# Shared gate-up weights split inside cross attention's last batch, and the router's choice of experts put ahead of the shared unit

## What the kernel computes

```python
shared = jax.nn.silu(x @ Ws_gate) * (x @ Ws_up) @ Ws_down           # 512 -> 704 -> 512
scores = jax.nn.softmax(x @ W_router, axis=-1)                      # 8 experts
topk_vals, topk_idx = jax.lax.top_k(scores, 2)
combine = jnp.einsum('bsk,bske->bse', topk_vals, one_hot(topk_idx)) # weights of 2048 tokens
h = silu(einsum('td,edh->eth', xf, We_gate)) * einsum('td,edh->eth', xf, We_up)   # 352 wide
routed = einsum('etd,te->td', einsum('eth,ehd->etd', h, We_down), combine)
```

## Time and profile before

| | |
|---|---|
| median of three runs | 1088.21 us (1085.95 to 1089.79) |
| the profiled execution | 1088.47 us, of it 1086.8 us span |
| TensorE busy | 1016.1 us, 93% of the span |
| VectorE, ScalarE, GpSimd busy | 666.1, 456.7, 275.8 us |
| TensorE's granted clock | 0.974 of full speed, mean |
| cross attention's last batch | from about 512 to 551 us |
| `route` | 551.2 to 640.0 us |
| `experts`, `combine` | from 640.0 and from 927.7 us |

### The profile page before, as it was taken

How to read it: one execution, slowest core, us unless ns; L and a number is a source line. 1 busy time by engine, 2 the same in 40 slices (tenths; PEclk the granted TensorE clock), 3 DMA queues, 4 the chain that set the end, 5 groups by cost and what they waited for, 6 DMA issues and landing times. The chain is left out here.

```text
span 1086.8 us, 18081 instructions
## 1 busy us (share of the span) xinstructions
PE 1016.1 (93%) x6368; PEld 858.2 (79%) x6368; DVE 666.1 (61%) x1502; ACT 456.7 (42%) x798; POOL 275.8 (25%) x367
## 2 busy tenths in 40 slices
PE   7899999999979999999859979999999999899997
PEld 5688888888778888887637768888998889778785
DVE  4836556477265776776444847776777776253576
ACT  5623314145125544454443226555655664221110
POOL 4510100213143323333343122212231220503040
PEclk9999999999978999999998979999999999999999
DMA  5403032023877888884432157787778773615042
GB/s 168 180 1 116 0 115 87 0 81 126 205 187 194 212 228 239 218 219 131 171 99 81 63 179 225 252 256 266 243 246 277 251 244 113 213 40 188 6 155 77
DMA packets 87183, 172.66 MB, mean 159 GB/s; under 512 B 8112, under 2 KB 36016, under 8 KB 85328
## 3 DMA queue, kind: packets, MB, share of 16 engines
q1 hardware_dynamic: 81008, 150.08, 44.6%
q0 software_dynamic: 6112, 21.76, 6.1%
HBM read 130.92 MB, written 37.49 MB: 155 GB/s over the span
## 5 line engine op out<-in xcount | busy, mean ns | idle before, releaser
L45 PE MATMUL e_ps_h<-e_x_lo,e_gu_hi 128*128 128x256 f32 (+1 forms) x384 | 111.3, 290 | 10.8 <-DVE e_x_lo L2141 8.7
L45 PE MATMUL a_ps_proj<-region_a_rounded,arena 128*128 128x512 f32 x272 | 107.4, 395 | 11.2 <-DVE region_a_rounded L369 6.2
L953 DVE CUSTOM_DVE_ANT_0 b_dump<-b_ps_s,b_mask 128x128 f32<-128x128 f32 (+1 forms) x256 | 80.4, 354 | 46.5 <-PE b_ps_s L1143 43.3
L47 PE MATMUL e_ps_h<-e_x_hi,e_gu_hi 128*128 128x256 f32 (+1 forms) x384 | 108.2, 282 | 0.0
L46 PE MATMUL e_ps_h<-e_x_hi,e_gu_lo 128*128 128x256 f32 (+1 forms) x384 | 108.2, 282 | 0.0
L46 PE MATMUL a_ps_proj<-region_a_rounded,arena 128*128 128x512 f32 x272 | 106.4, 391 | 0.0
L47 PE MATMUL a_ps_proj<-region_a_rounded,arena 128*128 128x512 f32 x272 | 106.4, 391 | 0.0
L2147 DVE TENSOR_TENSOR e_gu_lo<-f_region_a,e_gu_hi 128x704 fp32r<-128x704 f32 x92 | 81.3, 889 | 26.8 <-ACT e_gu_hi L2057 26.3
L388 DVE SCALAR_TENSOR_TENSOR f_region_b<-a_ps_proj,a_taps,f_region_b 128x510 f32<-128x510 f32 (+2 forms) x96 | 71.7, 746 | 40.8 <-ACT f_region_b L328 38.5
L843 ACT ACTIVATE b_pt<-b_ps_x 128x384 f32<-128x384 f32 x128 | 61.8, 487 | 61.2 <-PE b_ps_x L1167 61.1
L757 POOL TENSOR_SCALAR_AFFINE_SELECT b_pt<-b_pt 128x256 f32<-128x256 f32 x128 | 51.8, 407 | 122.6 <-ACT b_pt L843 121.9
(11 more groups left out here) (400 smaller groups left out, 2693.7 us busy)
## 6 DMA issues: line engine op xcount, KB each, us to landing
f_region_a<-we_gate_up SPq DMA_DIRECT2D x88, 352.0 KB, 5.6
qk_split<-arena SPq DMA_DIRECT2D x24, 512.0 KB, 5.8
y_slots<-f_region_b SPq DMA_DIRECT2D x16, 512.0 KB, 3.4
f_x_next<-x SPq DMA_DIRECT2D x7, 1024.0 KB, 7.1
b_sk<-qk_split SPq DMA_DIRECT2D x24, 256.0 KB, 4.4
b_sq<-qk_split SPq DMA_DIRECT2D x24, 256.0 KB, 5.7
f_region_a<-we_down SPq DMA_DIRECT2D x12, 512.0 KB, 4.0
f_region_b<-we_down SPq DMA_DIRECT2D x11, 512.0 KB, 4.0
```

Of the source, the lines that this page charges most:

```text
L45: pe.matmul(out, a_hi, b_lo, start=first, stop=False)
L47: return pe.matmul(out, a_hi, b_hi, start=False, stop=last)
L953: ins = dve.tensor_tensor_reduce(dump[:, n % 2, cols], ps_s[:, n % 2, cols], mask[:, cols], -1.0, 3e38, ALU.add, ALU.min, peak[:, u, k, i: ...
```

## The change

Shared weights no longer have room of their own before `route`; they are laid over cross attention's arena, at places whose old content (query weights, key and value weights, split tiles) is dead when each is written. With that:

- SP, in batch 7, waits for batch 6's last scores, then issues shared parts 0 and 1 and both groups of x2, ahead of the store of batch 5's rows and of batch 7's peaks. Parts 2 and 3 follow behind the batch.
- ACT rounds parts 0 and 1 behind batch 7's last exponent, ahead of `keep`, and part 2 at the end. POOL takes their rests behind its last mask. Part 3 is rounded in `route` at (0, 1), and POOL takes its rest ahead of the constants but behind the root of the variance.
- The constants are waited for later, the first down part is fetched at `route`'s start.
- DVE picks both experts before it does unit 0's product; the counts follow unit 1 and not unit 2; units 1 to 3 are done within the chain of small instructions, unit 4 behind `hot_lo`, unit 5 behind `hot_hi` and its two multiplications, all adds behind that; the one-hot products stand ahead of down tile 2, not 3.
- The three table loads are taken out.

```diff
@@ cross_attention, SP
             for t in range(FIRST_T, END_T):
                 b = projected(t)
+                if t == B - 1:
+                    sp.wait_ge(e_ready, order(B - 2, 1, UH - 1) + 1)
+                    shared.load_part(sp, 0)
+                    shared.load_part(sp, 1)
+                    sp.wait_ge(xkq_ready, x_count(B - 1, 1))
+                    sp.wait_ge(normed_stored, 16 + 16 * (t - 2))
+                    sp.dma_start(xt[:], x2_dram[0]).then_inc(inputs_loaded[0], 16)
+                    sp.dma_start(own_b[:, 0:4 * GT]..., x2_dram[1]).then_inc(inputs_loaded[0], 16)
...
+            shared.load_part(sp, 2)
+            shared.load_part(sp, 3)
@@ cross_attention, POOL, at the end
+            for k in range(3):
+                shared.rest_part(pool, k)
@@ cross_attention, ACT
+                if t == B - 1:
+                    shared.round_part(act, 0)
+                    shared.round_part(act, 1)
                 keep(t)
             for u in range(2):
                 attended(B - 1, u)
+            shared.round_part(act, 2)
@@ Shared
+    def load_part(self, sp, k):
+        if k >= 2:
+            sp.wait_ge(self.part_lo_done, k - 1)
...
+    def round_part(self, act, k):
+        act.wait_ge(self.part_loaded[k % 2], 16 * (k // 2) + 16)
+        act.activation(hi, self.w_part[rows, k % 2, 0:cols], ACT.Copy).then_inc(self.part_hi_done, 1)
+    def rest_part(self, pool, k):
+        pool.wait_ge(self.part_hi_done, k + 1)
...
+        pool.tensor_tensor(lo, self.w_part[...], hi.bitcast(F32), ALU.subtract).then_inc(self.part_lo_done, 1)
@@ route, SP
             sp.dma_start(w_raw[:], w_router).then_inc(w_loaded, 16)
+            shared.load_part(sp, SPLIT + 1)
@@ route, POOL
             pool.memset(w_hi_lo[:].bitcast(F32), 0.0).then_inc(consts, 1)
+            pool.wait_ge(var_done, 1)
+            pool.tensor_tensor(ln.rstd[:], ln.var[:], ln.power[:], ALU.pow).then_inc(rstd_done, 1)
+            shared.rest_part(pool, SPLIT)
             pool.memset(before[:], 1.0).then_inc(consts, 1)
...
@@ route, ACT
-            act.preload_act_table_set("exp_and_others")
...
-                    if (g, c) in PARTS_AT:
-                        split_part(PARTS_AT[g, c])
+                    if g == 0 and c == 1:
+                        shared.round_part(act, SPLIT)
@@ route, DVE
-            shared.up(dve, 0, 0)
+            dve.wait_ge(iotas, 14)
...
             dve.tensor_tensor(both[:], pick[:, 0], pick[:, 1], ALU.add).then_inc(sub_both_done, 1)
-            shared.up(dve, 0, 1)
-            shared.up(dve, 0, 2)
+            shared.up(dve, 0, 0)
...
             link(dve.tensor_tensor(hot_lo[:], ...))
+            shared.up(dve, 0, 4)
             link(dve.tensor_tensor(hot_hi[:], ...))
-            dve.wait_ge(x2_stored, 16)
-            shared.add(dve, kept, 0, 0)
             for k in range(2):
                 rows = hot_hi[:, k * NT:(k + 1) * NT]
...
+            shared.up(dve, 0, 5)
+            dve.wait_ge(x2_stored, 16)
+            for t in range(TILES):
+                if t == 2:
                     dve.wait_ge(placed, 1)
@@ route, PE
-                if u == 2:
+                if u == 1:
                     pe.wait_ge(sub_both_done, 2)
...
-                if t == TILES - 1:
+                if t == 2:
                     pe.wait_ge(hot_done, 2)
@@ experts, ACT; combine, ACT
-            act.preload_act_table_set("silu_and_others")
```

More of the change, by code:

```diff
@@ L515, in cross_attention @@
 def cross_attention(nc, x1_dram, ctx_t, weights, x2_dram, left_ln, ident, xt, c_raw, res, ln, spare, c_hi, c_lo, split_dram,
-                    rounded, own_a, own_b, ws_gate_up):
+                    rounded, own_a, own_b, shared):
     with ExitStack() as ctx:
@@ L735, in _ @@
                     load_stack(t + 2, 1)
-            sp.wait_ge(xkq_ready, x_count(B - 1, 1))
+            shared.load_part(sp, 2)
+            shared.load_part(sp, 3)
             sp.wait_ge(normed_stored, 16 + 16 * NORMED)
[L738 to L744, removed]
+            sp.wait_ge(inputs_loaded[0], 32 * (GROUPS - 2) + 32)
         @block.gpsimd
@@ L1306, with __init__ @@
 class Shared:
-    def __init__(self, sb, sem):
+    ROOM = 2 * DC * 2 * DS + 2 * S_UNITS * D + 2 * 3 * P + P
+    def __init__(self, room, w_part, w_gate_up, w_down, sem):
         U = S_UNITS
[L1313 to L1316, removed]
+        chunk, down = [P, 2 * DS], [P, U, D]
+        hi, lo = [None] * DC, [None] * DC
+        hi[0], lo[0] = room("s_gu_hi_0", chunk), room("s_gu_lo_0", chunk)
+        self.dn_hi = room("s_dn_hi", down)
+        hi[3] = room("s_gu_hi_3", chunk)
+        self.small_hi, self.small_lo = room("e_small_hi", [P, 3, P]), room("e_small_lo", [P, 3, P])
+        room("s_gap", [P, P])
+        for c in (1, 2):
+            hi[c], lo[c] = room("s_gu_hi_%d" % c, chunk), room("s_gu_lo_%d" % c, chunk)
+        lo[3] = room("s_gu_lo_3", chunk)
+        self.dn_lo = room("s_dn_lo", down)
+        self.gu_hi, self.gu_lo = hi, lo
+        self.w_part = w_part
+        self.parts = self.list_parts(w_gate_up, w_down)
+        self.part_loaded = [sem("s_part_loaded_even"), sem("s_part_loaded_odd")]
+        self.part_hi_done = sem("s_part_hi_done")
+        self.part_lo_done = sem("s_part_lo_done")
         self.x_ready = sem("s_x_ready")
@@ L1326, in __init__, with list_parts @@
         self.out_free = sem("s_out_free")
-    def parts(self, w_gate_up, w_down):
+    def list_parts(self, w_gate_up, w_down):
         every = slice(0, P)
-        out = [(self.gu_hi[:, c], self.gu_lo[:, c], every, 2 * DS, w_gate_up[:, c]) for c in range(DC)]
+        out = [(self.gu_hi[c], self.gu_lo[c], every, 2 * DS, w_gate_up[:, c]) for c in range(DC)]
         for u in (0, 2):
@@ L1608, in _ @@
                 n += 2
[L1609 to L1613, removed]
+            for k in range(SPLIT + 1, S_PARTS):
+                shared.rest_part(pool, k)
             pool.wait_ge(token_known, 1)
@@ L1649, in _ @@
                 if DC + u < S_PARTS:
-                    split_part(DC + u)
+                    shared.round_part(act, DC + u)
         @block.vector
@@ L1730, in of_experts @@
                 return row.rearrange("p (o e) -> p o e", o=1).broadcast_to([P, NT, E_N])
+            shared.product(dve, 0, 1)
             link(dve.tensor_scalar(odd_base[:], first[:, 1], twice[:], float(P), ALU.add, ALU.mult))
@@ L1735, in _ @@
             link(dve.tensor_tensor(spill[:], spill[:], odd_base[:], ALU.subtract))
+            shared.rest(dve, 0, 1)
             link(dve.scalar_tensor_tensor(spill[:], spill[:], -float(SLOTS * SINGLES), over[:], ALU.add, ALU.mult))
@@ L1747, in _ @@
             link(dve.tensor_tensor(pos[:], pos[:], cand[:], ALU.add))
+            shared.product(dve, 0, 2)
             for k in range(2):
@@ L1750, in _ @@
                 link(dve.tensor_reduce(slot_f[:, k], cand[:], AX_X, ALU.add))
+            shared.rest(dve, 0, 2)
             def of_turns(x):
@@ L1756, in of_ends @@
                 return ends[:, k].rearrange("p (o e) -> p o e", o=1).broadcast_to([P, E_TILES + 1, E_N])
-            shared.product(dve, 0, 3)
             link(dve.tensor_copy(rt.slot[:], slot_f[:]))
```

80 lines of the change are left out of this document (34 added, 46 removed).

## The result

The change makes the kernel slower by 6.1 us. Before: 1087.56 us, median of 13 runs (1084.29 to 1091.32). After: 1093.64 us, median of 13 (1090.25 to 1098.44). The ratio is 1.0059, interval 1.0039 to 1.0079. The profiled execution of the changed kernel took 1091.24 us (span 1089.5). The forecast was 1088.6 us, "same", range to 1092.5: 5.0 us too low, and 1.1 us outside the range.

A forecast was written before the change was run, and what follows sets the result against it. TensorE was busy 93% of the span, but ScalarE's queue and a DMA ended last in the router. Terms +3.0 - 5.5 + 4.6 - 1.2 - 0.5 = +0.4 on 1088.2 gave 1088.6 us, range 1082.5 to 1092.5.

The forecast's parts named there:

- r_lo and tail: Cross attention's tail: GpSimd's queued second rest holds VectorE's r_lo to 540.9 for 537.9, +3.0 us.
- router: Router stage: x's rounding no longer waits, but a rest delays the normalisations; hidden units start 5.5 us earlier.
- hidden units to experts: First hidden product to the next block: 62.3 us for 57.75, through units 4 and 5's new place, +4.6 us.
- table load, experts: Load removed before the experts' first weight rounding: -1.2 of its 1.28 us arrives.
- table load, combine: Load removed in combine, where the first chunks are turned by 928.9: -0.5 of 1.28 us arrives.
- the locks: GpSimd's rests hold VectorE operations with two SBUF inputs or normalising: terms of 3.0, 2.4 and 4.4 us.
- one low stretch at 1.5 us: Down tile: TensorE at low clock after its gap, first eight products 3.5 us for 1.9, added as 1.5 us.
- the 5.76 us: TensorE gap in the old router, behind ScalarE's queue, where a rounding waited for a transfer 5.02 us too late.
- 62.3 us: First hidden product to the next block: 60.8 us plus 1.5 for low clock, against 57.75 before.
- VectorE's chain: Shared stage, counts to hot rows: starts 13.5 us after the first hidden product, ends 33.1 to 33.2, before 37.7.
- "+6": Upper bound of the term from hidden units to experts, with two low stretches, where the forecast was +4.6 us.
- rival (a): GpSimd gives way: queued rests wait for VectorE, the three lock terms go, -9.4, 1079.2 us; chance 0.31.

The follow-up runs named there:

- the fillings: Changed kernel with unread TensorE products inside waits: down tile's two 1089.4 us (ratio 1.0024), router's 1088.45 us (1.0003), both 1084.86 us (0.9971).

## Why the prediction was wrong

Against the mean of three profiles each, the terms of the sum came out so:

```
                              forecast   measured
r_lo and tail                   +3.0       +4.5
router                          -5.5       -4.3
hidden units to experts         +4.6       +6.0
table load, experts             -1.2       -1.3
table load, combine             -0.5       -0.6
sum                             +0.4       +4.3
experts' stage itself            0         +2.0
```

The signs were right in every line, and so were the locks, the waits and the gaps. Two steps failed. The low clock behind the new waits was put at nothing for r_lo's and the router's, and at too little in the down tile. And the lengths of the kernel before came from one execution.

**The clock behind new waits.** I priced one low stretch at 1.5 us, behind unit 5, from the row of a wait of 1.85 us, and none behind r_lo's wait or the router's. In the router the forecast was 25.5 us from its first product to the first hidden one; with the wait filled it takes just that, 25.50, and unfilled 26.6 to 28.0. So the lock's own cost there was right and the low clock of 1.1 to 2.5 us was missing. In the down tile the clock costs 2.83 us for the forecast 1.5. By the times of whole kernels the fillings gave 3.0, 5.3 and together 8.8 us, each with 3 us of uncertainty. Behind r_lo's wait the changed kernel has 6.8 low us in all three profiles (0.80 in its first window), the kernel before 3.4, 0 and 0; this one was not filled. With r_lo's lock taken away the tail takes 14.5 us, 1.7 more than the kernel before on the mean, of which `a_lo`'s meeting with part 1's rest explains 0.8; the rest, beside a low stretch of 3.4 us, is not separated. The forecast's own rows held the warning, since eight products at the low level stand behind the 5.76 us.

**The base.** The lengths came from one execution, the best one could do then, but I took the waits and low stretches in it as belonging to the kernel. Two more profiles show the same stages 2.9 us shorter. From the first hidden product to `experts` I forecast 62.3 us, and measured were 62.0, 63.6 and 62.0; it was compared with 57.8, while the other two profiles have 56.0. Likewise the tail: with a base of 12.2 the changed kernel loses 5.1 us and not 3.5.

**Luck.** The 62.3 is closer than its parts. VectorE's chain was to reach hot_lo 33.1 us behind the first hidden product and unit 5's rest to end at 44.7; in the first profile they come at 31.0 and 42.6, because the chain's first copy starts at 11.9 and not 13.5 and the rest of the chain is a little shorter too. From unit 5's rest to `experts` it takes 19.4 us and not 17.6, mostly for the clock. The two errors cancel. The rise of 6.0 us in this term is also the "+6" which the prediction gave for two low stretches, but it comes from the base.

**The locks** were forecast well: r_lo +3.0 (3.0), the normalisations to 4.60 us, the rests of parts 5 to 7 in the chain 2.1 + 1.1 + 1.0 = 4.2 us (4.3). Holding GpSimd back at r_lo and at the normalisations removes the first two; the three in the chain are read from the rows alone, where each held operation ends with a rest. The Trainium skill's rule ("SBUF — State Buffer", "Who interferes with whom") therefore held, and rival (a), GpSimd gives way, is refuted. Its time was also added up wrong: 9.4 below 1088.2 is 1078.8 us, and the 1079.2 counts the +0.4 twice.

**What stays open.** The mean span of the changed kernel's three profiles is 5.7 us longer, near the 6.1 of the medians. It is not 4.3 + 2.0 alone: what stands ahead of r_lo is 0.5 longer, and `combine` as a whole 1.7 shorter, of which only 0.6 is in the table above. The +2.0 in the experts' stage has no cause that I could show. Its instructions are the same, and over all profiles it took 281.2 to 288.5 us, the kernels with a filled wait at 281.2 to 282.5, but that with the table loads at 281.8 too, and that with r_lo freed at 288.5. Three profiles of each are too few to call it part of the change. The share of the table loads is known only as 1.6 to 2.9 us.

## What to carry to other kernels

Work moved to an idle engine is not free when its operations hold up those of a busy one: give GpSimd's long subtractions a wait that lets VectorE's next critical operation pass first, as the two waits here did, which cost two lines.
A new wait of TensorE can cost more than its length, by the low clock behind it: here 2.8 us behind two waits of 3.3 and 4.1 us, and 1.1 to 2.5 us in the router behind one of 4.8. Where a wait can't be removed, products that nobody reads can keep the clock.
Before adding up seams of a few us, profile the same kernel more than once: three identical executions differed by 2.9 us in the very stages that decided this case.

## What had not been expected of the hardware

Products into an unused PSUM bank, 19 in a wait of 4.76 us and 30 in waits of 3.28 and 4.13, made the kernel 8.8 us faster by the ratios, with 3 us of uncertainty, although no left-over came sooner by them (TensorE could take up unit 5 42.7 us behind the first hidden product in the changed kernel, and 45.5 in the kernel with the down tile filled, whose hidden units had a low stretch of their own).
Operations of 8 and 24 columns were held for a whole rest of GpSimd (2.26 and 1.16 us for 0.17), so the size of an operation is no protection.
The three profiles of the changed kernel have the same low stretch of 10.2 us behind the down tile's waits, each starting 7.4 to 7.8 us behind the first down product, but the one at the first hidden products in one of them only; those behind the changed kernel's waits of 3.19 to 4.76 us were there every time, the others come and go between executions.
